# GpSimd issues its gathers in two runs of four and waits for each run to land

## The reference

```python
# layer 0, run twice (STEPS = 2)
edge_feat  = concatenate([h[src], h[dst]], axis=-1)
messages   = relu(edge_feat @ msg_W1 + msg_b1) @ msg_W2 + msg_b2
att        = sigmoid(relu(edge_feat @ att_W1 + att_b1) @ att_W2 + att_b2)
aggregated = segment_sum(messages * att, dst)
h          = mlp(concatenate([h, aggregated])) + h + global_repr

# layer 2 (8 heads)
attn = einsum('ehd,ehd->eh', Q[dst], K[src]) * rel_scale[edge_type] / sqrt(16)
w    = exp(attn - max(attn));  w = w / segment_sum(w, dst)[dst]
out  = segment_sum(w[..., None] * V[src], dst) @ Wo + bo
```

## Time and profile before

| | us |
|---|---|
| median of three runs | 7089.4 |
| span of the profiled execution | 8961.2 |
| POOL busy in it | 4865.9 |
| PE busy in it | 5673.7 |
| DVE busy in it | 4867.9 |

### The profile page before, as it was taken

The page is one execution under the profiler, slowest core; times in us unless marked ns, Lnnn a source line. Parts: engine busy times, 40 slices in busy tenths (PEclk is TensorE's granted clock), DMA queues, the critical chain, the costliest instruction groups (busy, mean ns, idle before and its releaser), DMA issues. The chain is left out here.

```text
span 8961.2 us, 134318 instructions
## 1 busy us (share of the span) xinstructions
PE 5673.7 (63%) x28658; PEld 4800.1 (54%) x28659; DVE 4867.9 (54%) x17338; ACT 1151.3 (13%) x3238; POOL 4865.9 (54%) x4715
## 2 busy tenths in 40 slices
PE   6555556677777767777768778656666665333334
PEld 5555555466666556666655555456666663333333
DVE  6555554455555545555557777545555553444555
ACT  1111111111111111111112222100000001000001
POOL 2566564555555355555527888445454451566664
PEclk6555555777777877777779999865655556555556
DMA  5334434333333233333324444333333332333332
GB/s 154 95 95 97 94 94 126 92 97 93 95 93 96 57 102 94 94 97 98 94 53 67 69 69 69 78 83 88 89 89 87 89 89 37 77 75 75 74 77 49
DMA packets 930244, 770.85 MB, mean 86 GB/s; under 512 B 586631, under 2 KB 762899, under 8 KB 928115
## 3 DMA queue, kind: packets, MB, share of 16 engines
q0 software_dynamic: 245936, 426.87, 19.9%
q1 hardware_dynamic: 675276, 329.60, 14.6%
q10 hardware_dynamic: 8960, 13.52, 0.6%
HBM read 681.88 MB, written 86.32 MB: 86 GB/s over the span
## 5 line engine op out<-in xcount | busy, mean ns | idle before, releaser
L1180 POOL DMA_INDIRECT there<-table_wide,idx x1664 | 1597.4, 960 | 1396.8 <-DVE prod L1203 615.9
L1271 PE MATMUL ps<-here,hot_t 128*128 x3328 | 1238.1, 507 | 631.3 <-DVE there L1222 599.7
L2288 POOL DMA_INDIRECT there<-table_wide,idx x832 | 792.7, 953 | 902.6 <-DVE msg L2364 434.8
L1222 DVE TENSOR_TENSOR there<-there,ps 128x512 f32<-128x512 f32 x832 | 571.2, 687 | 1169.8 <-remote 607.7
L1271 PEld LDWEIGHTS ps<-here,hot_t 128*128 128x128 f32 x3328 | 740.9, 247 | 756.5 <-issue 668.9
L2677 POOL DMA_INDIRECT there<-table_narrow,idx x832 | 791.3, 951 | 649.5 <-issue 259.1
L693 POOL DMA_INDIRECT rec<-out_recd,posd x806 | 817.5, 1014 | 564.4 <-issue 263.9
L1279 PE MATMUL ps<-relu,hot_s 128*128 128x128 f32 x3328 | 878.0, 356 | 140.3 <-DVE hot_s L1211 108.1
L2837 PE MATMUL ps<-here,hot_t 128*128 x1664 | 434.5, 436 | 803.6 <-DVE prod L2758 419.3
L1947 POOL DMA_INDIRECT partial_sums<-row_sums1a,idx1a x504 | 814.9, 1617 | 167.4 <-issue 147.3
L1279 PEld LDWEIGHTS ps<-relu,hot_s 128*128 128x128 f32 x3328 | 688.5, 238 | 326.3 <-issue 272.1
(11 more groups left out here) (486 smaller groups left out, 9773.3 us busy)
## 6 DMA issues: line engine op xcount, KB each, us to landing
locrows<-loc_row SPq DMA_DIRECT2D x416, 256.0 KB
krowd<-key_row SPq DMA_DIRECT2D x201, 256.0 KB
there<-table_wide,idx POOLq DMA_INDIRECT x2496
src_rows1a<-slot_src_row SPq DMA_DIRECT2D x42, 768.0 KB
lrowd<-lo_row SPq DMA_DIRECT2D x201, 128.0 KB
attr_raw<-in_edge_attr SPq DMA_DIRECT2D x201, 128.0 KB
there<-table_narrow,idx POOLq DMA_INDIRECT x832
rec<-out_recd,posd POOLq DMA_INDIRECT x806
```

The lines of the kernel that those rows point to most:

```text
L1180: nc.gpsimd.indirect_dma_start(there[:, j, q, :], None, table, bass.IndirectOffsetOnAxis(idx[:, j, q:q + 1], 0)).then_inc(gathered[j][q], 16)
L1222: nc.vector.tensor_tensor(pair, pair, ps[:, WORK, :], ALU.add).then_inc(summed, 1)
L1271: last = nc.tensor.matmul(ps[:, WORK, (q % 2) * 2 * F:(q % 2 + 1) * 2 * F], hot_t[:, j % 2, q * P:(q + 1) * P], here[:, :, :].rearrange("p ...
L2288: nc.gpsimd.indirect_dma_start(there[:, j, q, :], None, table, bass.IndirectOffsetOnAxis(idx[:, j, q:q + 1], 0)).then_inc(gathered[j][q], 16)
```

## The change

After every fourth gather of a group (`q` = 3 and `q` = 7; `U // 2` is 4) GpSimd waits until each gather of this run of four has landed, and then raises `admitted` once more. `i * 16 + 16` is the value that `gathered[j][r]` reaches when the gather just issued has landed. The same four lines are added in both functions.

```diff
@@ -1179,6 +1179,10 @@
                         pool.sem_inc(admitted, 1)
                         nc.gpsimd.indirect_dma_start(there[:, j, q, :], None, table,
                                                      bass.IndirectOffsetOnAxis(idx[:, j, q:q + 1], 0)).then_inc(gathered[j][q], 16)
+                        if q % (U // 2) == U // 2 - 1:
+                            for r in range(q + 1 - U // 2, q + 1):
+                                pool.wait_ge(gathered[j][r], i * 16 + 16)
+                            pool.sem_inc(admitted, 1)
 
         @block.vector
         def _(dve):
```

## The result

The kernel with the change takes 8698.6 us (median of four runs, 8691.5 to 8718.0), the kernel before beside it 7088.8 us. The ratio is 1.228 (95% interval 1.226 to 1.230): 1610 us slower. Forecast were 8390 us, with a range of 7950 to 8680. The direction and the mechanism held, the price was 24% more than forecast (1610 against 1301 us), and the time lies 19 us outside the range.

The account below looks back on a forecast made before the run. POOL's gather issue was taken as nearly the bound, 10.3 us per group; two runs of 3.75 + 2.75 + 0.78 us make 14.56, so 312 x 4.26 = 1329 us on 7089.4 gives 8418, said as 8390, range 7950 to 8680.

Parts of the forecast that it names:

- What bounds the kernel: Layers 0 and 2: POOL's issue, 1.25 us per gather, nearly sets the pace unprofiled; 10.0 to 10.4 us per group, 10.3 taken.
- my forecast of the changed kernel's span, 9100 us: Profiled execution: layer 0 groups go from 13.9 to 14.56 us, +140 us on 8961; layer 2 has cover.
- That no slack hides the wait: Layers 0 and 2: POOL has no slack, the four-group ring doesn't help; 4.26 us more per group, 1329 us in all.
- The size of a run: POOL, four gathers: pitches, landing and restart take 7.28 us, so a group takes 14.56 us against 10.3.
- the restart: POOL, from the released semaphore to the next gather's start: 0.78 us, semaphore instructions' price included.
- start to landing: POOL, from the fourth gather's start to its landing being seen: 2.75 us taken, between 0.95 and 4.0.
- The signs in the profile: POOL idles some 2.6 us after every fourth gather, about 1600 us; idling on DVE goes; DVE's lines 1222 and 2322 await gathers.
- The ring covers the landing: Rival, layers 0 and 2: groups take 13.9 and 15.3 us unprofiled too; not slower, 7089, at worst 140 us more; 3%.
- The landing quick or the slack larger: Rival: landing of 1.85 us gives 7857, or a group of 11.3 us before gives 8106; 14%.
- PE slow as well: Rival, layers 0 and 2: PE at its low clock no longer overlaps fully, 1 us more per group, 8730; 12%.
- The waits do wait for this run's landing: Answers the rival that the waits wait for nothing, the number being an old landing's: time 7089; 1%.
- nothing became faster: Answers the rival of a faster kernel: fewer gathers collide and DVE's 2.35 us of "remote" would go; 1%.

Follow-up runs that it names:

- before_again: The kernel before, unchanged, profiled a second time, on one of the slower chips (B): 8970.2 us, span 8968.0.
- before_third: The kernel before, unchanged, profiled once more, on one of the faster chips (A): 7088.4 us, span 7086.3.
- last_only: The change, but POOL waits only for the fourth gather's landing of each run, one semaphore: 9169.9 us against 8963.8 for the kernel before, chips B.
- sp_free: The change, with SP starting the next group's rows before waiting for this group's gathers: 8722.1 us against 7090.1 for the kernel before, chips A.
- run8: The change with one wait per group, after the eighth gather: 8693.5 us against 8963.8 for the kernel before, chips B.
- run2: The change with four waits per group, after each second gather: 10933.2 us against 8973.8 for the kernel before, chips B.

## Why the prediction was wrong in size

**What bounds the kernel: right number, wrong cause.** I took the 1872 us between the profile's span and the median for the profiler's doing. They are a difference between the two kinds of chips (`before_again`, `before_third`). The working stood nevertheless, because it asked what no chip could shorten, POOL's own issue of 1.25 us per gather: 10.3 us per group was the forecast, 10.05 and 10.4 are measured. For the same reason my forecast of the changed kernel's span, 9100 us, compared two kinds of chips and says nothing of the measured 8716.2. On chips B, where it would apply, `last_only` took 9170 us, and its three semaphores less are worth some 70 us; by that estimate 9100 would have been 140 us short there.

**That no slack hides the wait: right.** A group is longer by all that POOL stands still, and the ring of four doesn't help: 628, 626 and 594 us of idling before the gathers that follow a wait, less the 0.3 us each that stand before any gather, are 1658 of the 1662 us by which the passes grew. Next to nothing is left for a cost of another engine.

**The size of a run: this step failed, in the restart.** Forecast 3.75 + 2.75 + 0.78 = 7.28 us for a run of four; measured 15.56 / 2 = 7.78 us in layer 0 and 15.36 / 2 = 7.68 in layer 2. By terms, as means over the trace of the change (landings and restarts over the 284 runs of layer 0 and the 207 of layer 2 that have a landing in it):
- the three pitches: 3.75 forecast, 3.80 and 3.86 measured. Most are 3.75, as from 2614.47 to 2618.22, some longer (2606.50 to 2610.54: 4.04);
- start to landing: 2.75 forecast, 2.80 and 2.84 measured, median 2.76. Nearly right, from a pair of rows of another gather with narrower rows; that it carries over so well was partly luck.
- the restart: 0.78 forecast, 1.2 and 1.0 measured. The 0.78 us of the earlier trace rows counts from the last of POOL's waits to the gather. With the change more instructions stand behind the landing. I had written that their price was "within the restart"; it was not.

What they cost can be read singly, because the restart is the same each time. After the fourth gather of a group it is 0.774 us with one semaphore and no other wait (`last_only`, layer 2), which is the forecast's 0.78. The other three semaphores make it 0.892 (the change, layer 2). The old waits for `cut` and `dotted` with their register instructions, which stand behind the landing only in layer 0, make it 1.125 (the change, layer 0). After the eighth gather it is 1.14 in layer 0 and 1.01 to 1.07 in layer 2, and where the loop body starts anew, once in eight runs, 1.60 and 1.36.

**The sum.** Over 0.78 us the restart has 0.41 us x 416 + 0.23 us x 208, some 220 us of the 309 that were missing. Landings and pitches have about 40 us each. The group before took 10.05 us in layer 0 and 10.4 in layer 2 instead of the 10.3 I took, which is 42 us more of a difference. The forecast was also lowered by 28 us on a guess that a landing is quicker unrecorded; no run shows that. Against these stand the 52 us by which the times differ less than the passes do (1610 against 1662) and 16 us that dividing a pass by 104 leaves out.

**The signs in the profile.** POOL's idling on DVE all but went (62.7 us in layer 0), and the pitch in a run stayed 1.25 us. POOL idles 3.0 us after every fourth gather in layer 0 and 2.9 in layer 2, 1848 us in all, where 2.6 and 1600 were forecast. One sign was wrong: line 1226 (1222 before) waits for gathers only twice, 2.3 us in all, since DVE waits for the late rows in that time; only `sp_free` brings that wait out. And the upper end of 4.0 us for a landing, "2.75 and half of it again", should have been 4.1.

**The rule on the price of a DMA.** The Trainium skill, "DMA: Bandwidth & Descriptors", section "Anatomy of one DMA — SWDGE (gpsimd) path", gives about 2.0 us plus bytes over 436 GB/s, by which 128 KB are an estimate of 2.3 us. The trace has a median of 2.8 us for these gathers: going by the row was right.

**The rivals.** The ring covers the landing: excluded on chips A by 1.228. The landing quick or the slack larger: neither, 2.8 and 10.05 us. PE slow as well: PE's granted clock did fall in layer 0. On chips A the windows of layer 0's first pass have it at 0.97 before and 0.76 after (span of the window, busy times by engine, clock, DMA share, GB/s):

```profile
1275.00:2325.00 1050.00, 847.14 (x4950) 710.61 (x4948) 800.30 (x3293) 201.46 (x512) 792.93 (x832) 0.97 0.46 130
```

```profile
1276.00:2895.00 1619.00, 1073.95 (x4988) 922.68 (x4987) 797.70 (x3320) 202.96 (x516) 792.65 (x832) 0.76 0.30 84
```

But the 0.5 us per run is not PE's: the next gather starts 1.125 us after the landing of the fourth in layer 0, the same in every group, which leaves no room for a wait on PE, ACT or DVE. The time came near this rival's 8730 for another reason. The waits do wait for this run's landing, and nothing became faster on chips A.

## What to carry to other kernels

A wait for a landing on the engine that issues the next transfers costs the full way, start to landing and restart, at every wait, as soon as that engine has no slack; the number of waits sets the price and hardly the number of semaphores (12.9, 15.5 and 20.7 us per group with one, two and four). If such a wait is needed, wait for the run before the one just issued: nearly the same waits, each for the run before, cost nothing on chips A (1.000) and 0.6% on chips B. And before a profile's idle time is taken for slack, compare its span with the times to be predicted: where they differ, work out what each loop can't go below, and count every instruction that will stand between the released wait and the next transfer.

## What the hardware showed that I had not expected

The same program takes 26% longer on chips B. From first to last transfer that GpSimd issues, the sort loop takes 1355 instead of 1048 us, a group of layer 0 13.9 instead of 10.05, one of layer 2 15.3 instead of 10.4, and layer 3 1290 instead of 1073 us. Layer 1 takes the same, 967 and 965 us, though GpSimd scatters beside a busy PE there too. PE's clock isn't the reason everywhere: in the sort loop it is granted 0.50 on both, and PE and DVE are busy there for the same time within 1%. In layer 0 DVE has pauses in most groups whose end the trace puts down to something "remote":

```profile
L1222 DVE TENSOR_TENSOR there<-there,ps 128x512 f32<-128x512 f32 x832 | 571.2, 687 | 1169.8 <-remote 607.7
```

The trace of the kernel before on chips B also has no landing of any of these gathers, as if records were missing. What the cause is, and whether it lies in the chip or in how it is recorded, stays open.

On these chips one wait per group makes the kernel faster by 3% (`run8`, twice). Of the 258 us between the two spans on one chip, 247 are in the gathers of layer 2. Their first and last start, before and with one wait:

```profile
L2288 POOL DMA_INDIRECT there<-table_wide,idx x832: 943/949/2165, 5830.9 to 7415.0; - x167
```

```profile
L2292 POOL DMA_INDIRECT there<-table_wide,idx x832: 943/949/2347, 5827.2 to 7164.1; - x167
```

1336.9 / 104 = 12.9 us per group is about POOL's pace with one standstill, 1348.5 / 104 = 13.0 on chips A. In layer 0 the same wait gains nothing: the first pass takes 1452.3 us against 1448.8, and the "remote" pauses are still there (790.1 us). With two waits per group (`last_only`, 2.7 us of "remote" left) and with four (`run2`, none) they are gone from layer 0:

```profile
L1225 DVE TENSOR_TENSOR there<-there,ps 128x512 f32<-128x512 f32 x832 | 569.1, 684 | 682.5 <-PE ps L1274 656.9
```

There the waits cost more than the pauses did. Why the pauses go was not tested. On chips A one wait per group is 12% slower, so the sign of such an edit can depend on the chip; no version beat the kernel before on both.
